# One chunk of expert outputs worked inside the router table's stage, a piece with each pair of blocks

## The reference, cut to what matters

```
out = segment_sum(msgs, dst).reshape(n, H * C) + bias          # third layer: sums, then a layer norm
x = x + ((out - mu) / sqrt(var + EPS) * gamma + beta)
x = layernorm(x)                                               # fourth layer
h = x @ W_gat                                                  # 16 router features and 2 x 4 attention terms a node
scores = layernorm(attention sums of h over the router edges)
for ei in range(4):
    hh = gelu(x @ W1[ei] + b1[ei])                             # 256 -> 512
    out = out + gate[ei] * (hh @ W2[ei] + b2[ei])              # 512 -> 256
```

## Time and profile before

| | us |
|---|---|
| median of 3 runs | 10487.33 (10477.21 to 10490.65) |
| the profiled execution's own time | 10549.46 |
| its span, first to last instruction | 10547.3 |
| router table's stage, first fetch to last scatter | 8253.7 to 8555.3 |
| expert stage, first matmul to last output | 8570.2 to 10202.4 |
| POOL's 1,024 row fetches in it | 8584.6 to 10093.0 |
| finish and choice | 10202.4 to 10547.3 |

### The profile page before, as it was taken

The page is one execution under the profiler, slowest core; times in us unless marked ns, Lnnn a source line. Parts: engine busy times, 40 slices in busy tenths (PEclk is TensorE's granted clock), DMA queues, the critical chain, the costliest instruction groups (busy, mean ns, idle before and its releaser), DMA issues. The chain is left out here.

```text
span 10547.3 us, 83890 instructions
## 1 busy us (share of the span) xinstructions
PE 7308.9 (69%) x22345; PEld 4293.4 (41%) x22345; DVE 6105.9 (58%) x17158; ACT 3382.3 (32%) x7429; POOL 5112.9 (48%) x5326
## 2 busy tenths in 40 slices
PE   2446655555668999999984566566656369889865
PEld 1322322222335555555562333332333245555544
DVE  9956666666666555555455677777777631222234
ACT  1223333333333333333342333333333331222123
POOL 0066666666651000003436666666666556666622
PEclk9767677777779999999996667767766569999987
DMA  3166665656651000001255566565656532222237
GB/s 115 57 198 186 186 191 183 190 186 188 190 176 50 25 24 25 25 23 33 22 124 172 182 189 187 184 190 186 187 184 189 157 105 52 61 57 54 61 107 236
DMA packets 672268, 1353.98 MB, mean 128 GB/s; under 512 B 203627, under 2 KB 402126, under 8 KB 670898
## 3 DMA queue, kind: packets, MB, share of 16 engines
q0 software_dynamic: 238688, 579.40, 21.8%
q1 hardware_dynamic: 406480, 743.56, 20.2%
q10 hardware_dynamic: 26626, 25.65, 0.7%
HBM read 711.27 MB, written 649.65 MB: 129 GB/s over the span
## 5 line engine op out<-in xcount | busy, mean ns | idle before, releaser
L1371 PE MATMUL g1sm_sump<-g_acc,g1sm_to 128*128 128x264 f32 x3520 | 1549.9, 564 | 1023.9 <-DVE g_acc L1517 647.1
L1371 PE MATMUL g0sm_sump<-g_acc,g0sm_to 128*128 128x260 f32 x3520 | 1506.1, 547 | 1036.1 <-DVE g_acc L1517 403.6
L1261 POOL DMA_INDIRECT g_acc<-htab,g1sm_src x1760 | 1672.5, 950 | 993.0 <-issue 677.3
L1261 POOL DMA_INDIRECT g_acc<-htab,g0sm_src x1740 | 1655.5, 951 | 903.1 <-issue 619.3
L1371 PEld LDWEIGHTS g1sm_sump<-g_acc,g1sm_to 128*128 128x128 f32 x3520 | 744.4, 254 | 1776.9 <-issue 1230.6
L1371 PEld LDWEIGHTS g0sm_sump<-g_acc,g0sm_to 128*128 128x128 f32 x3520 | 716.3, 247 | 1778.7 <-issue 1037.2
L803 POOL DMA_INDIRECT re_rerows<-rtab,re_resrc x1024 | 988.0, 965 | 520.8 <-issue 287.7
L1540 DVE SCALAR_TENSOR_TENSOR g_acc<-g_acc,g0sm_side,g0sm_sump 128x260 f32<-128x260 f32 x1705 | 816.1, 479 | 426.7 <-DMA side<-g_acc 202.4
L2409 DVE SCALAR_TENSOR_TENSOR g_acc<-f_yp,f_wgt,g_acc 128x256 f32<-128x256 f32 x784 | 342.6, 479 | 970.2 <-PE f_yp L2329 879.6
L1290 ACT ACTIVATE g1sm_to<-k_iota,g1sm_side 128x128 f32<-128x128 f32 x1760 | 559.4, 388 | 1029.7 <-DMA side<-g_acc 513.7
L1517 DVE TENSOR_TENSOR g_acc<-g_acc,g0sm_weightp 128x256 f32<-128x256 f32 x1760 | 727.8, 414 | 268.4 <-remote 149.0
(11 more groups left out here) (452 smaller groups left out, 9618.6 us busy)
## 6 DMA issues: line engine op xcount, KB each, us to landing
sums<-g_acc SPq DMA_DIRECT2D x440, 528.0 KB
sums<-g_acc SPq DMA_DIRECT2D x440, 520.0 KB
z<-k_arena SPq DMA_DIRECT2D x96, 512.0 KB
k_arena<-z SPq DMA_DIRECT2D x33, 1024.0 KB
g_acc<-htab,g1sm_src POOLq DMA_INDIRECT x1760
g_acc<-htab,g0sm_src POOLq DMA_INDIRECT x1740
x<-g_acc POOLq DMA_DIRECT2D x48, 512.0 KB, 3.4
re_rerows<-rtab,re_resrc POOLq DMA_INDIRECT x1024
```

The costliest lines, as they stand in the source:

```text
L1261: nc.gpsimd.indirect_dma_start(slot[a][:, u, :], None, table, bass.IndirectOffsetOnAxis(ap=src[a][:, u:u + 1], axis=0)).then_inc(landed[a] ...
L1371: nc.tensor.matmul(sump[u % BANKS][:, 0:W], to[u // LOT % RING][:, u % LOT, :], slot[a][:, u, 0:W], start=True, stop=True).then_inc(summed, 1)
```

## The change

Chunk 0 (blocks 0 to 3) leaves the expert stage: its four experts are worked in the router table's stage. A new class `FirstExperts` cuts that work into 32 units: four "hidden" units an expert (one quarter, two matmuls of 512 columns) and four "output" units (one block, four matmuls of 256 columns). PE works one unit after the `multiply` of each pair from pair 8 to pair 39. Four Gelus follow together on ACT once the fourth quarter of an expert is there, DVE takes two blocks of output at a time, and SP stores each expert's outputs to `z` in one transfer of 512 KB. The turned pairs 0 and 1 stay in a tile of their own and are no longer written to `turned`.

For the PSUM that this needs (four banks of hidden sums, two of outputs), `xTp` and `hp` are single tiles now: `turn` of a pair waits for `copy_xT` of the pair before it, `multiply` for `copy_h` of the pair before it. For the space in SBUF, the ring of fetched sums holds 56 blocks (28 pairs) instead of 84.

The expert stage has 24 chunks. The edges have groups of `G` = 50, 20 of them and a rest of 24, and `LAG` is 4. The lots of a group, five or six transfers long before, are six or seven long.

```diff
-    G, LAG = 46, 3
+    G, LAG = 50, 4
...
-        self.NG = NCH - self.LAG
+        self.NG = NCH - FirstExperts.COUNT - self.LAG
...
+class FirstExperts:
+    COUNT, BEGIN, PACE = 1, 8, 1
+    def __init__(self, nc, K, w, z, room):
...
+        done = [("hidden", 0, q) for q in range(self.HC)]
+        for t in range(self.COUNT * self.NE):
+            if t + 1 < self.COUNT * self.NE:
+                done += [("hidden", t + 1, q) for q in range(self.HC)]
+            done += [("output", t, q) for q in range(CHUNK)]
+        self.units = done
+        self.END = self.BEGIN + -(-len(done) // self.PACE)
...
+    def at(self, n):
+        a = (n - self.BEGIN) * self.PACE
+        return self.units[max(a, 0):max(a + self.PACE, 0)]
...
+    def hidden(self, pe, t, m):
+        i, e = divmod(t, self.NE)
+        if t > 0:
+            pe.wait_ge(self.h_done, (t - 1) * self.HC + m + 1)
+        for k in range(KC):
+            mm = self.nc.tensor.matmul(self.hp[m][:, :], self.w["w1s"][:, e, k, m * P:(m + 1) * P],
+                                       self.xT[:, k, i * self.NT:(i + 1) * self.NT], start=(k == 0), stop=(k == KC - 1))
+        mm.then_inc(self.h_ready, 1)
+
+    def output(self, pe, t, j):
+        e = t % self.NE
+        pe.wait_ge(self.h_done, (t + 1) * self.HC)
+        if j % 2 == 0 and t > 0:
+            pe.wait_ge(self.y_used, (t - 1) * 2 + j // 2 + 1)
+        for k in range(self.HC):
+            mm = self.nc.tensor.matmul(self.yp[j // 2][:, j % 2, :], self.hs[:, t % 2, k, j * P:(j + 1) * P],
+                                       self.w["w2s"][:, e, k, :], start=(k == 0), stop=(k == self.HC - 1))
+        if j % 2:
+            mm.then_inc(self.y_ready, 1)
+
+    def curve(self, act, t, m):
+        act.wait_ge(self.h_ready, t * self.HC + m + 1)
+        self.nc.scalar.activation(self.hs[:, t % 2, m, :], self.hp[m][:, :], ACT.Gelu,
+                                  bias=self.b1s[:, t % self.NE, m:m + 1]).then_inc(self.h_done, 1)
+
+    def take(self, dve, t, q):
+        if q == 0 and t >= 2:
+            dve.wait_ge(self.stored[t % 2], 16 * (t // 2))
+        dve.wait_ge(self.y_ready, t * 2 + q + 1)
+        self.nc.vector.tensor_tensor(self.zs[:, t % 2, 2 * q:2 * q + 2, :], self.yp[q][:, :, :],
+                                     self.w["b2s"][:, t % self.NE, :].unsqueeze(1).to_broadcast([P, 2, DIM]), ALU.add)\
+            .then_inc(self.y_used, 1)
...
-    KEPT = HELD * CHUNK // 2
+    KEPT = acc.shape[1] // 2
+    assert AHEAD <= KEPT
...
-        xTp = [c.ps(f"xTp{h}", [P, KC, 2, P]) for h in range(2)]
-        hp = [c.ps(f"hp{h}", [P, 2, C]) for h in range(2)]
+        xTp = c.ps("xTp", [P, KC, 2, P])
+        hp = c.ps("hp", [P, 2, C])
+        first.allocate(c)
+        rows_of = lambda n, k, j: xT[n % R][:, k, j, :] if n >= 2 * first.COUNT else \
+            first.xT[:, k, (2 * n + j) * P:(2 * n + j + 1) * P]
...
+                    for kind, o, q in first.at(n - FOLLOW - 1):
+                        if kind == "output" and q == CHUNK - 1:
+                            first.store(sp, o)
...
+                first.wait_weights(act)
                 for n in range(1, N + 8):
                     for step, lag in ((root, 1), (norm, 2), (store, 3), (root2, 4), (norm2, 5), (copy_xT, 6), (copy_h, 7)):
                         if 0 <= n - lag < N:
                             step(n - lag)
+                    for kind, o, m in first.at(n - FOLLOW + 1):
+                        if kind == "hidden" and m == first.HC - 1:
+                            for m in range(first.HC):
+                                first.curve(act, o, m)
...
-                    if n >= 2:
-                        pe.wait_ge(xT_copied, n - 1)
+                    if n >= 1:
+                        pe.wait_ge(xT_copied, n)
...
+                    for kind, o, q in first.at(n):
+                        if kind == "hidden":
+                            first.hidden(pe, o, q)
+                        else:
+                            first.output(pe, o, q)
...
+                    for kind, o, j in first.at(n - FOLLOW):
+                        if kind == "output" and j % 2:
+                            first.take(dve, o, j // 2)
...
+    COUNT = NCH - begun
...
-                for i in range(0, NCH - 2):
+                for i in range(0, COUNT - 2):
                     step(i, CHUNK, CHUNK)
-                step(NCH - 2, CHUNK, LAST)
-                step(NCH - 1, LAST, 0)
+                step(COUNT - 2, CHUNK, LAST)
+                step(COUNT - 1, LAST, 0)
 
...
+            held = 56
+            first = FirstExperts(nc, K, experts, z, acc[:, held:HELD * CHUNK, :].rearrange("p b w -> p (b w)"))
+            acc = acc[:, 0:held, :]
...
+                expert_outputs(nc, K, "f1", turned, z, experts, edges, room, FirstExperts.COUNT)
```

More of the change, by code:

```diff
@@ L1831, in _, with allocate, wait_weights, store @@
                     pool.wait_ge(stored[s], 16 * len(range(s, N, HS)))
-def finish_and_route(nc, K, name, acc, H, xin, xout, gamma, ws, table, keep, arena, sums, start, count, fill, starti, turned):
+class FirstExperts:
+    COUNT, BEGIN, PACE = 1, 8, 1
+    def __init__(self, nc, K, w, z, room):
+        self.nc, self.K, self.w, self.z = nc, K, w, z
+        self.NE, self.HC, self.NT = w["w1s"].shape[1], w["w2s"].shape[2], CHUNK * P
+        at, parts = 0, []
+        for n in (2 * self.HC * self.NT, 2 * CHUNK * DIM, KC * self.COUNT * self.NT):
+            parts.append(room[:, at:at + n])
+            at += n
+        self.hs = parts[0].rearrange("p (q k t) -> p q k t", q=2, k=self.HC)
+        self.zs = parts[1].rearrange("p (q j d) -> p q j d", q=2, j=CHUNK)
+        self.xT = parts[2].rearrange("p (k t) -> p k t", k=KC)
+        self.b1s = w["b1s"][:, :].rearrange("p (e k) -> p e k", e=self.NE)
+        self.zv = z.rearrange("(b p) f -> p b f", p=P)
+        done = [("hidden", 0, q) for q in range(self.HC)]
[5 more added lines that the diff above has]
+        self.END = self.BEGIN + -(-len(done) // self.PACE)
+    def allocate(self, c):
+        self.hp = [c.ps(f"ehp{m}", [P, self.NT]) for m in range(self.HC)]
+        self.yp = [c.ps(f"eyp{m}", [P, 2, DIM]) for m in range(2)]
+        self.h_ready, self.h_done, self.y_ready, self.y_used, self.z_ready = (c.sem("e" + n) for n in (
+            "h_ready", "h_done", "y_ready", "y_used", "z_ready"))
+        self.stored = [c.sem(f"estored{q}") for q in range(2)]
+    def at(self, n):
+        a = (n - self.BEGIN) * self.PACE
+        return self.units[max(a, 0):max(a + self.PACE, 0)]
+    def wait_weights(self, eng):
+        eng.wait_ge(self.w["w_in"], 16 * self.w["loads"])
+    def hidden(self, pe, t, m):
[27 more added lines that the diff above has]
+            .then_inc(self.y_used, 1)
+    def store(self, sp, t):
+        i, e = divmod(t, self.NE)
+        sp.wait_ge(self.y_used, t * 2 + 2)
+        sp.dma_start(self.zv[:, i * CHUNK:(i + 1) * CHUNK, e * DIM:(e + 1) * DIM], self.zs[:, t % 2, :, :])\
+          .then_inc(self.stored[t % 2], 16)
@@ L1840, in finish_and_route @@
+def finish_and_route(nc, K, name, acc, H, xin, xout, gamma, ws, table, keep, arena, sums, start, count, fill, starti, turned, first):
     D = DIM // H
-    N, R, AHEAD, LATE, TURNED = NB // 2, 4, 24, 8, 7
+    N, R, AHEAD, LATE, TURNED, FOLLOW = NB // 2, 4, 24, 8, 7, 8
+    assert first.END + FOLLOW < N
     C, TW = ws.shape[2], table.shape[1]
     assert NB % 2 == 0 and TW == C
-    KEPT = HELD * CHUNK // 2
+    KEPT = acc.shape[1] // 2
+    assert AHEAD <= KEPT
     held = lambda n: acc[:, n % KEPT * 2:n % KEPT * 2 + 2, :]
@@ L1891, in _ @@
                         load(n)
-                    if 0 <= n - TURNED < N:
+                    if 2 * first.COUNT <= n - TURNED < N:
                         m = n - TURNED
@@ L1901, in _ @@
                 for s in range(R):
-                    sp.wait_ge(xT_kept[s], 16 * len(range(s, N, R)))
+                    sp.wait_ge(xT_kept[s], 16 * len([n for n in range(s, N, R) if n >= 2 * first.COUNT]))
+                for q in range(2):
+                    sp.wait_ge(first.stored[q], 16 * (first.COUNT * first.NE // 2))
             @block.gpsimd
@@ L1958, in copy_xT @@
                     act.wait_ge(xT_ready, n + 1)
-                    if n >= R:
+                    if n < 2 * first.COUNT:
+                        nc.scalar.copy(first.xT[:, :, 2 * n * P:(2 * n + 2) * P],
+                                       xTp[:, :, :, :].rearrange("p k j t -> p k (j t)")).then_inc(xT_copied, 1)
+                        return
+                    if n - R >= 2 * first.COUNT:
                         act.wait_ge(h_ready, n - R + 1)
-                        act.wait_ge(xT_kept[n % R], 16 * (n // R))
-                    nc.scalar.copy(xT[n % R][:, :, :, :], xTp[n % 2][:, :, :, :]).then_inc(xT_copied, 1)
+                        act.wait_ge(xT_kept[n % R], 16 * len(range(n - R, 2 * first.COUNT - 1, -R)))
```

(13 more changed lines are left out.)

29 lines of the change are left out of this document (13 added, 16 removed).

## The result

The changed kernel takes 10,559.9 us (median of 4 runs, 10,549.2 to 10,580.7) against 10,484.9 for the kernel before: a ratio of 1.007, interval 1.0055 to 1.0085, so 73 us slower, 58 to 89. The forecast was 28 us slower.

The account below looks back on a forecast made before the run. No one engine bounds the router table's stage throughout; POOL's fetches with their halts pace the expert stage. Terms 2 + 24 + 2 = 28 us, carried to the median 10487, give 10515 us; range 10440 to 10575.

Parts of the forecast that it names:

- rival B: Router table's stage: PE stays at 1.2 GHz through the 32 units, 100 us there; 10570 to 10590 us, chance 0.12.
- Expert stage, forecast +2: Expert stage: 20 groups at 70.5 us, then 219 us for 32 counts, 1629 us against 1627 before.
- the price of a group: Expert stage: a group of 50 fetches costs 62.5 us of work and 8.0 us of halts, 70.5 us.
- the step's own high end: Expert stage: halts in the same share of the work (9.0 of 57.5), 72.3 us a group, 38 us more.
- The reason for going below it: Expert stage: longer lots outlast PE's 13.7 us, so short halts go away and long ones stay; 8.0 us a group.
- Router table's stage, forecast +24: Router table's stage: the moved units' terms sum to 40 us, of which 19/32 show, 24 us; bounds 0 and 100.
- The bursts and the takes: Router table's stage: four ACT bursts of table loads and Gelus, 15 us of waits; eight DVE output takes, 5.5 us.
- The PE term: Router table's stage: eight of 32 pairs at PE's low clock, 2.5 us too much each, 20 us; bounds 0 and 80.
- the hole: Router table's stage, 8341 to 8438: DVE, ACT and PE almost still; POOL sets its length, and 19 units lie behind it.
- Finish, forecast +2: Finish: scans of 24 columns instead of 12, 0.9 us for 28 scans, 2 us with the rest of that chain.
- C: Whole kernel: the units vanish behind POOL's transfers, the expert stage is POOL's, nothing shows; 10485 us, chance 0.18.
- A: Expert stage: PE is the pacemaker, losing 0.26 us a fetch; the removed chunk gives back 54.8 us; 10450 us, chance 0.30.

Follow-up runs that it names:

- e1: The kernel before, unchanged, profiled once more; 10,485.7 us in its profiled execution.
- e9: The changed kernel, unchanged, run again against the kernel before on another chip; 10,621.9 us against 10,546.5, ratio 1.007.
- e4: The changed kernel without the work of the 32 pieces on PE, ACT and DVE, stores kept and writing zeros; 10,541.6 us, ratio 1.0049.
- e3: The kernel before with all 25 chunks in the expert stage, but edge groups of 50 and a lag of 5; 10,598.5 us, ratio 1.0103.
- e10: The kernel before with POOL allowed 16 counts ahead of PE's outputs instead of 4; 10,573.6 us, ratio 1.0082.
- e11: The changed kernel with the edge groups of 46 of before and a lag of 2; 10,452.6 us, ratio 0.9958.
- e6: The kernel before with POOL allowed 16 counts ahead instead of 4, in the session at 9,337 us; 9,335.9 us, ratio 1.000.
- e2: The kernel before with POOL waiting at every second lot until its own fetches have landed; 10,410.9 us, ratio 0.9934.

## Why the prediction was right in sign and short in size

The measured 10,559.9 us lies inside the stated range (10,440 to 10,575), but 10 us above the forecast's own (10,495 to 10,550). That the range holds it is in part luck: its upper end was drawn to take in rival B, and B's mechanism (PE at the low clock throughout) didn't come.

**The account.** Each trace gives four numbers: what a group costs (first fetch to first fetch), what is left from the rest's first fetch to the last output, and their sum with the 14 to 15 us ahead of the first fetch.

| | groups | a group | counts left | time left | stage |
|---|---|---|---|---|---|
| before, and e1 | 22 of 46 | 66.5, 66.1 | 24 | 156, 153 | 1632, 1622 |
| changed, and e9 | 20 of 50 | 72.3, 72.5 | 32 | 213, 207 | 1673, 1670 |
| e4 | 20 of 50 | 72.2 | 32 | 212 | 1670 |
| e3 | 20 of 50 | 72.1 | 40 | 262 | 1718 |
| e10 | 22 of 46 | 66.1 | 36 | 237 | 1705 |
| e11 | 22 of 46 | 66.0 | 16 | 102 | 1570 |

From row to row (with the mean where there are two profiles) a count is worth 6.4 to 7.0 us, and a fetch with its halts costs 1.43 to 1.45 us in every row.

**Expert stage, forecast +2, measured +45.** The counts were right: 24 to 32, forecast +55, measured +57 (213 against 156). The step that failed is the price of a group. I took "8.0 us of halts" for a group of 50 and 70.5 us in all; it is 72.3, which in the sum's terms (1.25 us of work a fetch, all else halts) is 9.8 us of halts. That is the step's own high end (halts in the same share of the work, 72.3), and 20 times 1.8 us are 36 us, nearly the whole miss.

The sum's split into work and halts was itself off. POOL's fetches in the full groups, before and changed, with what it waited for:

```profile
L803 POOL DMA_INDIRECT re_rerows<-rtab,re_resrc x1013 | 977.6, 965 | 485.9 <-issue 286.0 <-DMA g1nt_x<-x 167.0 <-PE f_yp L2575 32.9
...
L803 POOL DMA_INDIRECT re_rerows<-rtab,re_resrc x1001 | 978.0, 977 | 468.6 <-issue 288.8 <-DMA g1nt_x<-x 165.1 <-PE f_yp L2685 14.7
```

A fetch is busy for 0.97 or 0.98 us on average and the next follows after 0.30, so unbroken fetches stand 1.27 to 1.28 us apart; the 1.25 was read from one pair. A group of 50 is then some 64.1 us of work and 8.1 to 8.3 of halts (changed, e9, e4, e3), a group of 46 is 58.5 and 7.3 to 8.0 (before, e1, e10, e11): the halts kept their share of about 13% of the work. The reason for going below it was half right. Halts under 3 us did shrink, from 3.3 and 3.7 us a group to 1.5 and 1.2 (the two profiles of either kernel), as the forecast said; but the longer ones grew by as much or more, from 4.7 and 3.9 us to 6.7 and 7.1. A lead of 16 counts left the halts as they were in e10, and where PE is not braked there are none (e6, the same kernel), so they come from PE's braking and not from how lots and outputs meet. Why their share is the same in every grouping isn't shown.

**Mechanism.** That a long run of POOL slows PE was argued from one run; e10 stretched that run to 150 us and PE's slow stretch with it, and e2 cut the runs and gave PE 5 us a chunk. That is shown for the sessions at 10,490 us. That PE is freed the moment POOL halts isn't so (15 us later in e10). What in the run brakes PE, and why it is absent at 9,337 us, stays open.

**Router table's stage, forecast +24, measured +14 or 15.** The bursts and the takes were right: an interval between divisions is 7.2 us with a burst instead of 3.75, 3.45 each (forecast 3.7), DVE waits 3.2 of them, and a take adds 0.6. The PE term (20 us at the low clock, 12 of them showing) can't be told apart in the trace. Ahead of the hole, at a mean clock of 0.60, it costs nothing: the divisions stay 3.74 to 3.79 us apart but for one burst. Right behind the hole it may well have come:

```profile
8400.00:8440.00 40.00, 34.78 (x122) 24.43 (x123) 25.93 (x103) 24.56 (x59) 27.91 (x27) 0.65 0.65 197
```

PE is busy 34.8 of 40 us at a mean clock of 0.65, ACT waits 1.1 to 4.5 us before most copies of its products, and seven intervals between divisions from 8405.4 on take 41.7 us instead of 26.2, one burst among them. But the kernel before has such intervals behind its hole too (4.43, 6.59 and 10.72 us), with PE idle in them. From 8447 on a pair with its unit fits in 3.74 us at 1.00. The sum of 14 or 15 us is what is shown; how it divides between bursts, takes and PE isn't. The hole is there in every trace of these sessions; how much of the bursts it hides differs from one to the next (326.9 to 332.8 us for the stage with pieces).

The Trainium skill's page "ScalarE: Activation LUTs", section "What ACT_TABLE_LOAD costs", adds a drain of about 1380 ns to each load. The timeline above disagrees again: the loads end at 8469.99 and 8473.72, and the next ACTIVATE begins within 0.02 us.

**Finish, forecast +2.** Not to be told apart from the scatter of two profiles each.

**The rivals.** C (nothing shows) is out by e4 and e3. B (PE at 1.2 GHz through all units) is out by the clock. A said that the chunk gives back its 54.8 us of PE. Its mechanism was 0.26 us of PE a fetch in any grouping; then a group of 50 would take 54.8 + 13 = 67.8 us, under its own mark of 69. It takes 72.3, so PE loses 0.35 us a fetch there and 0.25 in groups of 46: what stays the same is POOL's time a fetch, not PE's loss. And e3, where A has no difference, costs 108 us. Yet with the groups kept (e11) the chunk's time does come back as A said, 52 to 63 us of stage and 44 of the kernel. What made the change slower is not the moved chunk but two groups fewer: e3 has that part alone, and costs 108 us.

## What to carry to other kernels

Where one engine's stream is paced by a gate on another's progress, ask first how much is left behind the last gated lot: here each count left was worth 6.4 to 7.0 us at the end, and 20 groups of 50 leave 32 counts where 22 groups of 46 would have left 16. Price a longer lot by the measured cost of a fetch with its halts (1.45 us), not by the work plus a hoped-for saving. And a halt that the program chooses can be cheaper than one that it runs into: e2's waits took POOL 1 us a group more than the old halts and let PE do 9% more in the same time, but the same kind of wait cost 1% where nothing braked PE, so it has to be measured where the kernel will run.

## What the runs showed of the hardware that was not expected

Indirect transfers that POOL starts back to back can nearly stop TensorE's issue: one MATMUL every 2.8 us through 120 us, with data there, no semaphore waited for, and the DMA share at 0.11 (e10). It began some 22 us into POOL's run of 150 us and ended 15 us after POOL's last fetch, with nothing issued by POOL and a DMA share of 0.00 in between; behind runs of 31 to 50 us PE was mostly back in 3 or 4 us.

The same kernel on the same chip took 9,337 us in one session and 10,494 in another, 12% apart, each within 0.3% of itself. In the quick one POOL's fetches and a full PE ran side by side for 1,306 us (e6), and the hole in the router table's stage was gone too. What decides it isn't known from these runs.

A wait for landings costs POOL 2.1 us behind its last fetch (e2), about what eight small memsets in a row take.
